# Five lines of jobs on one core: the turns of each engine in another order

## The reference: what is computed

```python
x = x + L0_attn(_layernorm(x))   # spiking attention, 16 heads, softmax over 256 positions
x = x + L0_ffn(_layernorm(x))    # gated FFN, all operands quantised to FP4 in blocks of 16
x = x + L1_attn(_layernorm(x))   # 4 Mamba blocks: conv, projections, a scan over time of 256 x 16 states
x = x + L1_ffn(_layernorm(x))    # ternary weights, hidden size 512
x = x + L2_attn(_layernorm(x))   # causal linear attention, 16 heads
x = x + L2_ffn(_layernorm(x))    # top-1 of 8 experts, all eight computed and masked
x = x + L3_attn(_layernorm(x))   # per-channel convolution as a scan, projection, layernorm
x = x + L3_ffn(_layernorm(x))    # dense FFN plus product-key retrieval of experts
```

## Time and profile before

| | |
|---|---|
| three runs | 1856.01, 1857.85, 1848.19 us; median 1856.01 |
| span of the profiled execution | 1849.7 us |
| DVE busy | 1499.8 us (81%) |
| PE busy | 1481.9 us (80%) |
| ACT busy | 1345.1 us (73%) |
| POOL busy | 1196.0 us (65%) |

### The profile page before, as it was taken

How to read it: one execution, slowest core, us unless ns; L and a number is a source line. 1 busy time by engine, 2 the same in 40 slices (tenths; PEclk the granted TensorE clock), 3 DMA queues, 4 the chain that set the end, 5 groups by cost and what they waited for, 6 DMA issues and landing times.

```text
span 1849.7 us, 27473 instructions
## 1 busy us (share of the span) xinstructions
PE 1481.9 (80%) x9417; PEld 1054.5 (57%) x9417; DVE 1499.8 (81%) x2326; ACT 1345.1 (73%) x2733; POOL 1196.0 (65%) x999
## 2 busy tenths in 40 slices
...
DVE  6589999999999899978898888888889999731254
...
GB/s 194 1 69 70 121 18 95 113 70 103 115 117 119 126 104 110 72 69 24 64 119 123 117 127 134 92 112 49 127 136 141 132 104 70 66 33 85 115 18 6
DMA packets 84585, 170.10 MB, mean 92 GB/s; under 512 B 9440, under 2 KB 14944, under 8 KB 84064
## 3 DMA queue, kind: packets, MB, share of 16 engines
...
...
## 4 chain that ended last, share of the span: by engine, by line
PE 42%; DVE 22%; ACT 19%; POOL 7%; issue 6%; DMA 3%; SPq 1%; DVEq 0%; POOLq 0%; ACTq 0%
DVE m L1051 8%; ACT m L1026 6%; DVE dtuB L1043 5%; PE ps L1080 4%; PE ps L1182 4%; PE ps L1467 3%; PE ps L1476 3%; PE ps L1314 3%; PE ps L965 3%; DMA m<-m 3%; PE ps L1764 3%; ACT L347 2%; PE ps L698 2%; PE ps L1325 1%; PE ps L711 1%
## 5 line engine op out<-in xcount | busy, mean ns | idle before, releaser
L1061 POOL TENSOR_TENSOR m<-m 128x1024 f32<-128x1024 f32 x256 | 777.2, 3040 | 162.8 <-DVE m L1051 161.1
L1051 DVE TENSOR_TENSOR_SCAN m<-m,dtuB 128x1024 f32<-128x1024 f32 x256 | 584.5, 2283 | 22.7 <-ACT m L1026 9.3
L1026 ACT ACTIVATE m<-m,Aneg 128x255 f32<-128x255 f32 x1024 | 431.7, 499 | 26.0 <-DMA m<-m 18.2
L1043 DVE TENSOR_TENSOR dtuB<-m 128x1024 f32<-128x1024 f32 x256 | 348.9, 1363 | 9.7 <-DMA m<-m 3.2
L1467 PE MATMUL ps<-o 128*128 128x256 f32 x512 | 150.8, 406 | 17.9 <-DVE X L1411 7.1
L1080 PE MATMUL ps<-m,w_const 128*32 128x256 f32 x2048 | 154.6, 432 | 12.1 <-POOL m L1061 12.1
L1434 ACT ACTIVATE o<-ps,w_mo 128x256 f32<-128x256 f32 x256 | 114.8, 472 | 54.9 <-PE ps L1467 54.0
L364 POOL TENSOR_TENSOR o<-o,mhalf 128x2 f32<-128x2 f32 x64 | 19.6, 306 | 200.0 <-DVE o L358 199.9
L965 PE MATMUL ps<-m,wc 128*128 128x256 f32 x512 | 134.3, 421 | 7.4 <-ACT m L385 7.3
L1476 PE MATMUL ps<-o 128*128 128x128 f32 x1024 | 130.6, 281 | 4.9 <-ACT o L1434 4.1
L1476 PEld LDWEIGHTS ps<-o 128*128 128x128 f32 x1024 | 124.5, 195 | 14.8 <-ACT o L1434 9.5
...
## 6 DMA issues: line engine op xcount, KB each, us to landing
m<-m SPq DMA_DIRECT2D x256, 256.0 KB, 4.8
...
o<-in_mox SPq DMA_DIRECT2D x128, 256.0 KB, 2.9
...
w_l3f<-in_l3f SPq DMA_DIRECT2D x1, 1536.0 KB, 17.5
...
```

The lines of the kernel that those rows point to most:

```text
L1026: op = e.activation(dA[at % NA][:, j, 1:CH], R[q][:, h * CH + 1:h * CH + CH], ACT.Exp, scale=Aneg[:, l, 4 * g + j:4 * g + j + 1])
L1043: e.tensor_tensor(dtuB[:, :, :], bc(R[q][:, (2 + h) * CH:(3 + h) * CH].unsqueeze(1), 4, CH), Br[k % 2], ALU.mult).then_inc(S.dve, n.tick(f ...
L1051: e.tensor_tensor_scan(flat(G[at % NG]), flat(dA[at % NA]), flat(dtuB[:, :, :]), 0.0, ALU.mult, ALU.add).then_inc(S.dve, n.tick(f"s{g}"))
L1061: e.tensor_tensor(G[at % NG], G[at % NG], Cr[k % 2], ALU.mult).then_inc(S.pool, n.tick(f"c{g}"))
```

## The change

Nothing but the strings of `ORDER` is changed. Each engine's string has the same number of turns of each line, and all instructions, waits, semaphores and buffers are the same. The first part of each string, and the last lines of three (a line of "..." marks what is left out):

```diff
     "pe":
-        "a9ua2ua3ba2ba7bab2ab8ab2ab2ab5a3bab2a2f2b3faf2bab2abasa4b2a3fa2f2af2sa2bab2abab2asb2fab4sfabfsaf2bfsb2fsab2af2af3"
+        "a17u2b2a5ba2bab10ab2a2b6a2ba2b2a2f2b3f2afasb3aba6fba3bfasf2afa2bab2a2b3absfsb5f2saf2bfba2b2sfbafaf2sfafsa3bab4aba"
...
     "dve":
-        "aua7u2bu3b7a11ba2fb2fb3a7b5fb2fs3fsbs2bs2bs4b2sb2fs8fs2af2s8a2sfa2fasf2s4as5a2sa2fs2abas2bs3a2bafasabababs2f2s6b"
+        "a8u3bu3b7a11ba2fb2fb3a6bab4fb2fs2fs10b2sb5fs8fs2f2s6as3a2fa2fsaf2s6as3a4sfs2a2s2bs2bsba2fa2safabafb2s8bsb4fs9fsf2"
...
-        "abab3a2bab2abab3aba2b2a2baba2b5a3b2a6b3a2b3ab3a2ba2b2a5b6ab3abab2ab",
+        "b4a4b2aba4b4aba2b4ab4",
     "act":
-        "a7u2a2ua2bua2ba2ba5bab3ab5ab2a2b6a3bafabf2abfb2f2afbab2a2sa2bfbsabasafsafs2asf2af2asb2absba2s2b2asb2s2bfbfbs2af4"
+        "a3ua7ba4u3baba6b4ab6aba2b6a3bafabf2abfb2f2afb2aba2sabfasafasbfas3asafbf2afasab2sab2sabs3b3sbfbfsasf3b2afbas2bfsaf"
...
     "pool":
-        "ua3ub2ubu2au2afbfau3afbfsfs4b2sfs5fs4asf2s5fsa2s2bas2fs4fs4fs5asb2f2bs5fs6fs5f2sfs7bfaf2s5fbs3afs3as2fs6fsabs3fs2"
+        "ua3b2u2bu2au5afbafafbfbfs5bsfs5fs5af2s5fsas2abafs5fs5fs5asbf2b2s5fs6fs5f3s8bfaf2s5bfs3afs2as3fs5fs2abs3fsbfs7fs2b"
```

More of the change, by code:

```diff
@@ L209 @@
     "sp":
[L210 to L213, removed]
+        "uf2s4fs4f3s8f3s12f2s4f4s8fsfs2fs5f2s2fs6f2s4fs4f3sa2s5a2sasa4f2sbabas7fb4f3s8b5a3f2sas4afs3a4f3s3as2a2s2a2sb2a2f3"
@@ L214 @@
+        "bs2bs3b2s3b5f2bfbs3b2s5bf2s8f3s8f4s8a4f2a2safs5asasa3f2b3s5bfs2bsbf2b2fs5bs3b3a3f2afa3s8a8b2fbafs8b2fb9s3fbfs2bs3"
+        "f4sa5sas4a6s9f3sb5fbf2s3bs2b2s2b2asba4f2afs8a4f3s8a3b2abf3sbsas2bs3b2asb5f2bs4bs2bfsbs2f2s3fs4a12b12a12ba2b4a2b11"
+        "ab",
     "pe":
-        "a9ua2ua3ba2ba7bab2ab8ab2ab2ab5a3bab2a2f2b3faf2bab2abasa4b2a3fa2f2af2sa2bab2abab2asb2fab4sfabfsaf2bfsb2fsab2af2af3"
-        "b2sa3bab2a2safbabasa5fafbfa2fsfa6sa2fasaf2b2sfafafb2sb2fa2fsfbf2bfb2sb8sb2afsb4fsf3bfbsfsa2bf3asf2b2asfa2sbababa2"
@@ L217 @@
[L217 to L225, removed]
-    "dve":
-        "aua7u2bu3b7a11ba2fb2fb3a7b5fb2fs3fsbs2bs2bs4b2sb2fs8fs2af2s8a2sfa2fasf2s4as5a2sa2fs2abas2bs3a2bafasabababs2f2s6b"
[L228 to L234, removed]
-        "abab3a2bab2abab3aba2b2a2baba2b5a3b2a6b3a2b3ab3a2ba2b2a5b6ab3abab2ab",
@@ L236 @@
-    "act":
-        "a7u2a2ua2bua2ba2ba5bab3ab5ab2a2b6a3bafabf2abfb2f2afbab2a2sa2bfbsabasafsafs2asf2af2asb2absba2s2b2asb2s2bfbfbs2af4"
[L238 to L248, removed]
@@ new lines @@
+        "a17u2b2a5ba2bab10ab2a2b6a2ba2b2a2f2b3f2afasb3aba6fba3bfasf2afa2bab2a2b3absfsb5f2saf2bfba2b2sfbafaf2sfafsa3bab4aba"
+        "sfa4bfa3bafa3bfsf2saba2ba5sfafafs2fafafb2sb2fa2bf3sf2b2sbab7sb2fb5sfsf4bsbfba2fbfsfsfabfasafababa2bfa2fafabfabfb2"
+        "s2aba2babsfasbfa2fabfaba2fafsa2bab2a6sbafbabafbafba2sfbsbfafb2a7ba2sb2a2faba2bfb2sbabfbafbfsfababa2ba2basba2fba6b"
+        "absa2fafba3fa2fabfsb3ab6absb5afab2ab2fsfa2bfsfb2afb3absb5fb2ab2afb2sb2fbafa3fabfsba4b2sab2fba2bsabfa3fa2fbabfa5fs"
@@ new lines @@
+        "a2b4a3ba4sab2afb3a2bf2bfaf2b2s2b9sb3fb2a4fb3fa3sbfsbfa2fb2a3sfbaba2sf2bafaf2asb4a4b3sfaba2fbfafsfa2bafa2basa2b2ab"
+        "a2basafb2fabfasafa2bfa2bafab2a2sa2ba2b2a2ba3b3a2sab3fa2b2a2ba3fba2bfbabsafba2fba2fsa2b2a2b2ab2ab2sbabfb3abfb2fb3f"
+        "ab2abfbabfbababab2ab3s2b2abab7sfa2bsa3f2bf3a4babsaba2b2a2b2a3safa4b2afbfb3afafbsfa5sa2b2a3ba2b2safab3fa2fbabfaf2"
+        "s2ab2ab2sab2afb2a2sfa3fba2fsf2a2baba2sbafababfsafb2a2fa2bfa2fbsb9sbafa2bafabfab2asafa2f2absb7a2b4asbafb2ab3fb2fb3"
+        "sa2bfb2fsafb6ab4sbabfb4sfa2fa2bafa2f2ba2saba3b2sbab2afabsa5b2a5b2a2b2aba2sa2b3ababsa3fa3ba3b2a2bab2a3babababab2ab"
@@ new lines @@
+        "aba5baba2b2aba2b2aba2b3a2b3a2b3aba2ba2b2a4ba2ba2ba2bab2ab2ab2ab5ab2ab2ab2abab5ab10ab7a2ba3ba2b5ababa4b2ab5a5b5",
+    "dve":
+        "a8u3bu3b7a11ba2fb2fb3a6bab4fb2fs2fs10b2sb5fs8fs2f2s6as3a2fa2fsaf2s6as3a4sfs2a2s2bs2bsba2fa2safabafb2s8bsb4fs9fsf2"
+        "s7as2a2sb2fafa2bfb4sb2fs11fsas8fs2f2s9a3f2afsfs2fsbs12fb2a2b2fbsf2sasafbasab3sbs6fb2s7abafsf2s3ba2basbas6fs8fs2f2"
+        "as2a2s2b2as5abfb2abs2fsaf2s10as2fsabsfs2babf2s2abs4as4abas2fabas2as2abafs2bf2s8bs3a4fabafa2bas3f2s2abs4a2b2s2asa3"
+        "ba2ba2fabs2b2sa3s6a2fs3a5f2a2fb4sb5s2b2s2bs3fb4sb3ab2sfsba2fb2fa2fab2sas4b3sb4s7afafasaf2s2a2s8asabas3bafbsb2fbsf"
+        "s2fs2bs6bsb3a2fsb2s6a2fabf2ab3s9fs6asfaf2as4b2a2s3ab2sbfs2bas4as2fs3af2s3as2b3as2bsfabs3a2sbsfa2f2bas2a2bs4bs3afa"
+        "basa5bas2asbsasb2fsaf2sfsa3ba2ba4b3a2fsas4a2s3b2a2bas2as4fb3fb2fbs2bfab2as5b5aba2b2afsbs4b3s3b2sf3s2bs2bs2abs4a2b"
+        "fs6fas2f2s2as5b2sas3fabfb2fsfs2bs2as8fs6afbf2s2babs6abs2bfs2bs4fabf2s2bs4bs6abafsbasasfabsfsfa2bsbs6a2baba3ba2fa"
+        "s2baba2s3a6sba2fbabsabfa2b2s2abab2s3aba2babs6b9asbasb2sabafa2fb5a4b2a2b4a2bab2abab3aba2b2a2baba2b4aba2b2a6b3ababa"
+        "b4a4b2aba4b4aba2b4ab4",
```

18 lines of the change are left out of this document (15 added, 3 removed).

## The result

The changed kernel takes 1892.45 us (median of 4 runs, 1888.67 to 1896.40), the kernel before in the same session 1856.93 (4 runs, 1848.19 to 1859.85). The ratio is 1.0205, with a 95% interval of 1.0172 to 1.0237: slower, and the interval leaves open whether by more than 2%. 1852.0 was forecast, and the range ended at 1880.

What follows compares the result with a forecast made beforehand. It took DVE, 89% busy from 107 to 1640 us, as the bound. +6.6 - 16 + 15 - 10 + 1 - 0.6 = -4.0 us on the 1849.7 span gave 1845.7, with 6.3 added 1852.0; range 1822 to 1880.

Steps and rivals of the forecast that it cites:

- The start: Up to the first scan at 107 us: a chain through all engines gets later by 6.6 us, bounds +2.0 and +8.7.
- the quantisation's last step: Setup's weight quantisation on DVE: its last step takes 1.36 us, free of POOL's L507, and ends at 26.1.
- The first scan: End of the start: the first L1043 would start near 113.6 us; at 107 or earlier the reading is wrong.
- The table loads: On ACT: 191 changes of set against 187, 5.1 us of ACT, counted as +1 us, bounds 0 and +5.1.
- The collisions: Rival, DVE and POOL waiting for each other at L1043 and L1061: doubled waiting would give 1885 us; chance 0.04.
- the sign that collisions decide: Over the kernel: DVE's busy time changing by over 10 us would show that collisions decide.
- The middle: 107 to 1640 us, DVE as bound: filled stalls -16, displaced producers +15, Front -10, table loads +1.
- Filled stalls: Middle: 20 DVE stalls filled by ready turns of other lines, -16 us, bounds 0 and -16.
- Displaced producers: Middle: turns that end DVE's stalls, 22 moved up (17.5 us), 21 moved behind others (32.4); net +15, bounds 0 and +32.
- Front: Middle: Front's turns, leading to the next unit's scan, come earlier on ACT, PE and DVE; -10 us, bounds 0 and -24.
- The end: Last 20 us: line a's two POOL products go ahead of b's chain; -0.6 us, bounds -3 and +3.
- The rival with the displaced producers in full: Turns releasing DVE cost +32.4 us in full and Front gains nothing: +24 on the span, 1880 us; chance 0.20.

Runs made afterwards that it cites:

- h1_start: New order on all engines from 0 to 107 us, the old one after, against the kernel before: 1858.38 us, ratio 1.0027.
- h10_1300: New order on all engines from 1300 to 1345 us only, against the kernel before: 1859.57 us, ratio 1.0051.
- h11_two: Old order with two short stretches of the new one, DVE from 1303.5 us and ACT from 1306.8 us, against the kernel before: 1861.01 us, ratio 1.0049.
- h15_1430: New order from 1430 to 1700 us only, against the kernel before: 1854.53 us, ratio 1.0009.
- r_h6: h6_rest once more, nothing changed, for a second profile; no time given; near 1421 us its distance rose by 0.5 us, in h6_rest by 7.4.
- h6_rest: New order on all engines from 1300 to 1430 us only, against the kernel before: 1866.48 us, ratio 1.0084.
- h14_1000: New order from 1000 to 1235 us only, against the kernel before: 1861.80 us, ratio 1.0059.

## Why the prediction was wrong

**The start was right.** Rows of the changed kernel that answer to the earlier trace rows:

```profile
24.69 1.32 DVE L410 TENSOR_TENSOR m<-m,o 128x1120 f32<-128x1120 f32 x1
29.77 1.94 PE L697 MATMUL ps<-o,o_vz 128*32 128x256 f32 x16 [4.15 <-ACT o L667]
33.70 1.28 ACT L576 ACT_TABLE_LOAD   x1
41.29 1.94 PE L697 MATMUL ps<-o,o_vz 128*32 128x256 f32 x16
115.79 1.23 DVE L1042 TENSOR_TENSOR dtuB<-m 128x1024 f32<-128x1024 f32 x1
```

The products were expected near 29.9 and at 41.7, the quantisation's last step at 1.36 us and its end at 26.1. They came at 29.77 and 41.29, 1.32 and 26.0. So the last step is free of the collision with L507, as said. The first scan was due near 113.6; it came at 115.79 and, in h1_start, at 114.20. There the distance of +7.4 is carried unchanged from 300 to 750 us and is +4 at 1250; the median of the runs is 5 us up.

**The table loads were right.** 192 (2737 instructions on ACT, 2733 before), where 191 or 192 were given. The switch has no further cost here either: the load of 33.70 ends at 34.98 and the sigmoid starts at 34.99. The Trainium skill (ScalarE: Activation LUTs, What ACT_TABLE_LOAD costs) adds a drain of about 1380 ns, and this trace doesn't show it.

**The collisions stayed out.** L1042's mean rose by 17 ns. DVE's busy time fell by 16.8 us, over the 10 us that I had set as the sign that collisions decide, but the kernel got slower: that test of mine took the busy time of DVE for the pace.

**What failed is the middle,** -10 us forecast (-16, +15, -10, +1) and about +30 in the trace. By its terms:

- *Filled stalls, -16.* This failed. I took DVE as the bound, so that each filled stall was a gain. The middle shows less busy DVE and more time. In h10_1300 the stall at the residual add is filled with two scans (1.7 us left of 6.0), and most of that is lost at L1119. There the stall was the sign of a late chain through line `b`, and filling it doesn't shorten the chain. That is one stall of the 20 counted; the others weren't tried one by one.
- *Displaced producers, +15, bounds 0 to +32.* The direction was right and the size too small. Two short stretches cost 9 us, although they put `b`'s turns behind only 3.5 us of others on DVE (1.23 + 2.28) and 4.0 us on ACT (0.60 and twice 1.70). The price of a displaced turn isn't the work put ahead of it. It is that, and all that its own lateness holds up in other queues: in h11_two `b`'s add 3.7 us late holds two transfers on SP, they hold the exponentials on ACT, these hold `b`'s norm. In the changed kernel the hold at this place is on PE and not on SP. I looked at one engine per move and never at SP, though its stretches that differ hold 327 turns.
- *Front, -10.* Front's turns do come earlier, and no stretch with them is faster than before. h15_1430 (1.0009) is the cheapest. No run moves Front's turns alone, so the term itself isn't measured.
- *The clock* had no term. It multiplies what the order starts: a stretch at 1.2 GHz where PE leads adds up to 7 us (r_h6 against h6_rest). The trace of before had it in view, with 0.89 in the long window of the earlier trace rows. How much of the 38 us it carries can't be split off. From 68 us on the profile of the changed kernel has 85 us more at the lower level; with PE busy four fifths of the time and half of that saved at the higher one, this is an estimate of 34 us of PE's work, next to the 33 us by which PE's busy time grew. Only part of it leads, and it is one pair of profiles: the kernel before alone differs by 18 us at the lower level between its two. So the clock may carry much of the loss, as a follower of the order. A kernel in which the order is new and the clock held was not made.
- *The end, -0.6, within 3 us.* It came out at +5 in one profile: 214.8 us from 1679 to the end, where 1640 to the end was 209.7. The share of the clock in that wasn't tried.

**The sum.** The rival with the displaced producers in full gave 1880, and it had named the way; it was still 12 us low. Without the -16 of the filled stalls it would be 1896, next to the 1892 measured, but that nearness is luck as far as the runs show: the sum has no term for the clock, and neither +32 nor 0 was measured for its parts. The rival had a chance of 0.20. Also, the device time is the span plus 1.9 us in each run that was profiled; the 6.3 us that I added were the distance of one execution's span from the median. That is right for a forecast of the median, but it isn't what lies around the span.

**What stays open:** what starts a fall of the clock at one execution and not at the next; which turns make the 11 us of h14_1000; by which queue most of the loss is passed on in the changed kernel, which was looked at in one place; and how much of the whole is clock.
